# Dilated attention with a head's two segments on separate halves of the partitions

## The chip, the cores and the metric

The kernel runs on one core of one Trainium2 chip. The metric is the device time of one execution in microseconds; the median of several executions is compared. The time before is 3458.81 us, the median of 3 runs (3457.89 to 3460.41).

## What is computed

Sixteen images of 128 channels and 28 x 28 pixels (784 tokens) go through a small hybrid network: two convolution blocks, a softmax attention, a routed block with GELU experts, a dilated attention, and a routed block with SiLU experts. The change is in the dilated attention and in the stage that prepares its operands. For each of 16 heads of 8 channels it computes three things on the tokens, in their order after a permutation:

```python
# tokens 0..255, dilation 1: softmax(q k^T / sqrt(8)) v over 256 tokens
# tokens 256..767, dilation 2: head h takes the 256 tokens of parity h % 2; the others give 0
# tokens 768..783 (all that is left of the third segment), dilation 4:
#                              head h takes the tokens of kind h % 4 (4 of 16)
o = out.transpose(0, 2, 1, 3).reshape(B, S, E)
return o @ w_out + b_out
```

So a head has two "segments" of 256 tokens with 256 x 256 scores each, and a rest of 16 tokens that is computed with a mask.

## The kernel before, in words

**Stage by stage.** `program` runs the stages one after the other on the residual `R`, which stays in SBUF. `dilated_inputs` (L1637) gathers the GELU experts' rows into `R`, normalizes, and multiplies by the q, k and v weights. `dilated_attention` (L1937) then runs the attention, with the routing of the following block woven into the same loop.

**Operands in pieces.** q and k are fp32 values written as three bf16 pieces each. One image's piece is 528 wide (`OWN = 2 * SEG + 16`): segment 0, segment 1 (a head's own parity), and the 16 tokens left. In `dilated_inputs`, TensorE writes the product into the PSUM tile `pqk` (`product`, L1782: two matmuls of 256 columns for parities, one for segment 0, one of 16 columns at L1786), ScalarE makes the first piece (L1849), VectorE the rest (L1907), ScalarE the second piece (L1852), GpSimd the third (L1751), and SyncE stores them to HBM (L1716). Between these, GpSimd gathers expert rows (L1739) and VectorE weighs them (L1866).

**Loads.** The attention works per image on tiles `q[side][g]` and `k_[side][g]`, where g is a group of 8 heads and the side alternates with the image. A tile has 99 partitions: six slots of 8 rows (products of pieces: hi x hi, hi x lo and so on, `Q_SLOTS` and `K_SLOTS`) are rows 0 to 47, rows 48 to 95 are zeros, and rows 96 to 98 hold three pieces of minus the row maximum in q, and ones in k. `load` (L2078) issues 12 DMAs on SyncE's queue for one (image, g), each 8 partitions x 8 heads x 528 elements (L2083). GpSimd zeroes k (L2131), VectorE zeroes q (L2341), ScalarE sets k's rows of ones (L2330).

**Units of one turn.** `steps` (L1953) writes out the order of the work of a turn by hand, for every engine alike; a turn has a step h for each head:

```python
for h in range(D_HEADS):
    score(2 * h)                 # also "weigh" and "take" of a group of 8 scores
    if maxima: out.append(("max", h))
    score(2 * h + 1)
    if maxima and h == 9: out.append(("turn", 0))
    if exps and h == 2:   out.append(("turn", 1))
```

- `score` k (L2191): the transposed scores of one (head, segment), two matmuls of 99 rows and 256 columns into one of three banks `sbank` (L2202), then the exponential on ScalarE (L2304). A bank comes free when its exponential is done. Before the change, unit k is head `4 * (k // 8) + k % 4`, segment `k // 4 % 2`.
- `max` h (L2205): the scores of the next image's head h, both segments, four matmuls of 96 rows (L2212) into one of two double banks `rot`, then a maximum along the rows on VectorE (L2360). Many other small steps share the two `rot` in turn: `turn`, `compact` (L2248), `den` (L2254), `add` (L2286), `rows` (L845, L846), `ranks` (L1008 on), `gate` (L1073), `score16` (L2260), `max16` (L2218), `weigh16` (L2270). TensorE waits for VectorE to free a `rot` before it fills it again (L2190).
- `turn` g (L2221): the maxima's pieces, made by GpSimd (L2146 to L2152), are transposed on TensorE (L2229, L2230), copied to `mt` by VectorE (L2366, L2367), and moved by three DMAs on SyncE into rows 96 to 98 of q (L2116).
- `weigh` gr (L2231): the context of four heads, 16 matmuls in fp32 with 32 output partitions each (L2241), copied by ScalarE (L2320).

A turn computes the scores of image t, the maxima of image t+1, and on SyncE the loads of image t+2: `load 0` at h = 8 and `load 1` at h = 15 (L2117), both behind waits for exponentials. Turn -1 has maxima alone. Score 0 of a turn waits for the max rows of group 0, score 16 and `score16` (at h = 5) for those of group 1. At the start SyncE issues the loads of two images, 48 DMAs, before anything else of its queue (L2090 to L2094).

## Time and profile before

| what | before |
|---|---|
| median of 3 runs | 3458.81 us |
| span of the profiled execution | 3455.1 us |
| what lies around the span, against the median | 3.7 us |
| dilated_inputs, from its first product to its last | 1995 to 2229 us |
| dilated_attention, first instruction to last exponential | 2240.4 to 3013 us |
| one image in the middle of it | 47.78 us |
| busy in such an image: TensorE, VectorE, ScalarE, GpSimd | 39.1, 36.3, 22.9, 28.4 us |

The span runs from the first to the last instruction of the profiled execution, and the sums of this document are made against it. Busy time of TensorE contains modelled pipeline ends, so it is more than what the array needs. Rows of the timeline name the engine (PE = TensorE matmul, PEld = its weight load, DVE = VectorE, ACT = ScalarE, POOL = GpSimd, SPq = SyncE's DMA queue), the line of the kernel, and in brackets how long the engine sat idle before and what released it ("issue": nothing that the profile shows).

### The profile page before, as it was taken

The numbers are of one execution on the slowest core, as the hardware profiler recorded it, in microseconds if no ns is written. First come the engines' busy times: TensorE is split into PE (matmuls) and PEld (weight loads), VectorE is DVE, ScalarE is ACT, GpSimd is POOL, SyncE is SP. The second block draws the span as 40 slices with busy tenths as digits, with TensorE's granted clock in tenths as the row PEclk, the third lists the DMA queues.
The fourth block names the chain that finished last, engine by engine and source line by source line (L and its number), as shares of the span: only waits on it lengthen the run. The fifth ranks groups of instructions, "written<-read, shape, count | busy, mean of one in ns | idle before, by whom it ended". The sixth has DMA issues, their size and how long they took to land. (4 is left out here: it accounts for less than half of the span.)

```text
span 3455.1 us, 64405 instructions
## 1 busy us (share of the span) xinstructions
PE 2842.9 (82%) x20886; PEld 1557.4 (45%) x20887; DVE 2208.0 (64%) x4232; ACT 1550.2 (45%) x3274; POOL 1023.2 (30%) x1344
## 2 busy tenths in 40 slices
PE   6777869999999999999499766578888888739998
PEld 3334523343333433333189655445555555423336
DVE  6774567778777787776222245477777777647662
ACT  1112526566666666666255422254444445414440
POOL 0001311122222222222333346425556565630000
PEclk9998969999999999999799889878898889859995
DMA  2002462223222232230222223332333233031123
GB/s 79 0 0 75 184 130 41 37 41 56 40 52 49 41 52 44 41 59 9 77 62 62 65 77 106 104 77 52 61 60 65 57 66 60 27 108 52 51 59 121
DMA packets 208898, 215.73 MB, mean 62 GB/s; under 512 B 33104, under 2 KB 184848, under 8 KB 208656
## 3 DMA queue, kind: packets, MB, share of 16 engines
q1 hardware_dynamic: 183024, 176.63, 22.3%
q0 software_dynamic: 14336, 25.72, 2.8%
q10 hardware_dynamic: 11312, 10.35, 1.0%
q8 instruction: 144, 2.36, 0.3%
q14 instruction: 82, 0.67, 0.1%
HBM read 129.26 MB, written 81.90 MB: 61 GB/s over the span
## 5 line engine op out<-in xcount | busy, mean ns | idle before, releaser
L1557 ACT ACTIVATE attn_exps<-attn_sbank 128x392 f32<-128x392 f32 x1600 | 705.0, 503 | 468.1 <-PE attn_sbank L1474 463.4
L1602 DVE TENSOR_REDUCE attn_mx<-attn_rot 128x1 f32<-128x784 f32 x768 | 722.4, 967 | 189.7 <-PE attn_rot L1487 186.7
L1487 PE MATMUL attn_rot<-attn_k,attn_q 96*128 96x392 bf16 x1536 | 402.7, 345 | 69.6 <-DVE attn_mx L1602 39.2
L1474 PE MATMUL attn_sbank<-attn_q,attn_k 99*128 99x392 bf16 x1536 | 451.2, 334 | 10.6 <-ACT attn_exps L1557 9.4
L2304 ACT ACTIVATE dil_exps<-dil_sbank 128x512 f32<-128x512 f32 x512 | 289.5, 598 | 365.0 <-PE dil_sbank L2202 361.6
L2360 DVE TENSOR_REDUCE dil_mx<-dil_rot 128x4 f32<-128x1024 f32 x256 | 307.4, 1218 | 74.0 <-PE dil_rot L2212 71.9
L1514 PE MATMUL attn_acc<-attn_exps,attn_v 128*32 128x392 f32 x3584 | 351.1, 503 | 0.0
L1474 PEld LDWEIGHTS attn_sbank<-attn_q,attn_k 99*128 99x128 bf16 x1536 | 149.2, 98 | 269.4 <-ACT attn_exps L1557 134.2
L2678 PE MATMUL silu_ph<-silu_route_w,silu_xT 128*128 x424 | 237.8, 645 | 20.4 <-issue 12.5
L1487 PEld LDWEIGHTS attn_rot<-attn_k,attn_q 96*128 96x128 bf16 x1536 | 117.8, 99 | 276.8 <-DVE attn_mx L1602 179.2
L2212 PE MATMUL dil_rot<-dil_k,dil_q 96*128 96x256 bf16 x1024 | 176.3, 302 | 80.2 <-DVE dil_mx L2360 50.4
L1105 POOL DMA_INDIRECT silu_rows<-silu_route_xt,silu_route_posi x224 | 213.0, 951 | 56.3 <-issue 54.0
L2202 PE MATMUL dil_sbank<-dil_q,dil_k 99*128 99x256 bf16 x1024 | 199.7, 300 | 13.6 <-ACT dil_exps L2304 12.1
L2729 DVE TENSOR_TENSOR silu_acc<-silu_h,silu_acc 128x512 f32 x212 | 146.8, 692 | 78.8 <-issue 46.1
L2702 ACT ACTIVATE silu_h<-silu_ph 128x512 f32<-128x512 f32 x212 | 126.6, 597 | 151.0 <-PE silu_ph L2678 151.0
L1429 POOL TENSOR_TENSOR attn_mx<-attn_mx_left,attn_own 128x4 f32<-128x4 f32 x32 | 6.5, 202 | 593.6 <-DVE attn_mx_left L1602 593.6
L2571 ACT ACTIVATE gelu_hT<-gelu_ph,gelu_wb 128x128 f32<-128x128 f32 x424 | 121.1, 368 | 109.3 <-PE gelu_ph L2545 109.3
L2212 PEld LDWEIGHTS dil_rot<-dil_k,dil_q 96*128 96x128 bf16 x1024 | 92.4, 104 | 158.2 <-DVE dil_mx L2360 92.3
L1514 PEld LDWEIGHTS attn_acc<-attn_exps,attn_v 128*32 128x32 f32 x3584 | 90.6, 109 | 150.5 <-issue 97.4
L2241 PE MATMUL dil_acc<-dil_exps,dil_v 128*32 128x256 f32 x2048 | 148.0, 439 | 1.4 <-ACT dil_exps L2304 1.4
L2593 DVE TENSOR_TENSOR gelu_y<-gelu_py,gelu_wb 128x128 f32<-128x128 f32 x106 | 30.9, 292 | 167.9 <-PE gelu_py L2555 167.9
L188 PE MATMUL conv_pb<-conv_z,conv_cw 96*128 96x392 f32 x192 | 89.3, 629 | 44.0 <-ACT conv_z L217 40.3
(367 smaller groups left out, 4789.8 us busy)
## 6 DMA issues: line engine op xcount, KB each, us to landing
attn_q<-q_pieces SPq DMA_DIRECT2D x192, 98.0 KB, 3.7
attn_k<-k_pieces SPq DMA_DIRECT2D x192, 98.0 KB, 5.1
silu_x<-silu_rows SPq DMA_DIRECT2D x212, 64.0 KB, 1.8
dil_q<-dil_q_pieces SPq DMA_DIRECT2D x192, 66.0 KB
dil_k<-dil_k_pieces SPq DMA_DIRECT2D x192, 66.0 KB
q_pieces<-qkv_piece SPq DMA_DIRECT2D x16, 588.0 KB, 3.1
k_pieces<-qkv_piece SPq DMA_DIRECT2D x16, 588.0 KB, 3.2
v_rows<-qkv_v SPq DMA_DIRECT2D x16, 476.0 KB, 3.8
```

The source lines that it names most:

```text
L1105: pool.indirect_dma_start(self.xs, bass.IndirectOffsetOnAxis(ap=self.posi[im.side][:, k, c:c + 1], axis=0), self.xt[im.side][:, c, :], Non ...
L1474: ins = nc.tensor.matmul(into[:, 0:HS], k_[t.side][g][:, j, c * P:(c + 1) * P], q[t.side][g][:, j, cols], start=True, stop=True)
L1487: ins = nc.tensor.matmul(rot[b][:, hf, 0:HS], q[nxt.side][g][0:QROWS, j, c * P:(c + 1) * P], k_[nxt.side][g][0:QROWS, j, cols], start=True ...
L1514: ins = nc.tensor.matmul(acc[32 * j:32 * j + 32, 0:HS], v[im.side][:, c, at:at + 32], e_[:, (u + (j if c < FULL else 0)) % NP, :], start=( ...
L1557: nc.scalar.activation(e_[:, n % NP, :], sbank[(n + t.side) % 3][:, 0:HS], ACT.Exp, scale=A_DIM ** -0.5).then_inc(s_ex, 1)
L1602: nc.vector.tensor_reduce(into, rot[b][:, :, 0:HS], AX.XY, ALU.max).then_inc(s_free, 1)
L2202: ins = nc.tensor.matmul(sbank[k % 3][:, kc * SEG:(kc + 1) * SEG], k_[t.side][h // 8][:, h % 8, at + kc * P:at + (kc + 1) * P], q[t.side][ ...
L2212: ins = nc.tensor.matmul(rot[b][:, seg, qc * SEG:(qc + 1) * SEG], q[nxt.side][h // 8][0:QROWS, h % 8, at + qc * P:at + (qc + 1) * P], k_[n ...
L2241: ins = nc.tensor.matmul(acc[32 * j:32 * j + 32, seg * SEG:(seg + 1) * SEG], v[im.side][:, 2 * seg + kc, at:at + 32], e_[:, (8 * gr + 4 * ...
L2304: nc.scalar.activation(e_[:, k % NP, :], sbank[k % 3][:], ACT.Exp, scale=D_DIM ** -0.5).then_inc(s_ex, 1)
L2360: nc.vector.tensor_reduce(mx[:, x[1], :], rot[b][:, :, :].rearrange("k s (q n) -> k (s q) n", n=SEG), AX.X, ALU.max).then_inc(s_free, 1)
L2678: nc.tensor.matmul(ph[n][:, :], xT[n][:], w1[:, bass.ds(e, 1), :].rearrange("p o f -> p (o f)"), start=True, stop=True).then_inc(s_ph, 1)
```

## The change

A head's segment 0 goes to partitions 0 to 63 and its segment 1 to partitions 64 to 127 of the q and k tiles. Each half has 48 rows of pieces and 3 rows for maxima or ones; the zero rows are gone. The 16 tokens left are stored behind both segments. Scores use 51 rows and maxima 48 rows of one half, so that each matmul starts at partition 0 or 64. Unit k is now head k // 2, segment k % 2. The loads become 24 DMAs per (image, g) of half the size, and the max rows 6 DMAs in place of 3. GpSimd sets the ones (and the rows that the loads then overwrite) with eight memsets; VectorE's four memsets and ScalarE's four instructions go. In `dilated_inputs` the two segments lie in two PSUM banks, and the product has one more matmul of 16 columns.

```diff
-OWN = 2 * SEG + 16
+HALF = SEG + 16
+OWN = 2 * HALF
...
-        rest = [[m.sb(f"rest{j}{t}", [P, OWN]) for t in two] for j in two]
-        piece = [[m.sb(f"piece{j}{t}", [P, PIECES, OWN], bf16) for t in two] for j in two]
+        rest = [[m.sb(f"rest{j}{t}", [P, 2, HALF]) for t in two] for j in two]
+        piece = [[m.sb(f"piece{j}{t}", [P, PIECES, 2, HALF], bf16) for t in two] for j in two]
...
                 def product(lhs, src, dst):
...
-                    return nc.tensor.matmul(dst[:, 2 * SEG:OWN], lhs[:, 0, :], src[:, 3 * SEG:S], start=True, stop=True)
+                    for seg in two:
+                        ins = nc.tensor.matmul(dst[:, BANK * seg + SEG:BANK * seg + HALF], lhs[:, 0, :], src[:, 3 * SEG:S], start=True, stop=True)
+                    return ins
...
-D_KR = QROWS + MROWS
+D_ROWS = 48
+D_KR = D_ROWS + MROWS
...
-        q = [[m.sb(f"q{s}{g}", [D_KR, 8, OWN], bf16) for g in two] for s in two]
+        q = [[m.sb(f"q{s}{g}", [P, 8, HALF], bf16) for g in two] for s in two]
...
-        LOADS = 16 * 2 * len(Q_SLOTS)
+        LOADS = 16 * 4 * len(Q_SLOTS)
...
                         for r, p in enumerate(slots):
-                            s = src[p, 64 * g:64 * g + 64, bass.ds(img.e, 1), :].rearrange("(h d) b s -> d h (b s)", d=D_DIM)
-                            sp.dma_start(dst[img.side][g][r * D_DIM:(r + 1) * D_DIM, :, :], s).then_inc(s_ld[img.side][g], 16)
+                            for seg in two:
+                                s = src[p, 64 * g:64 * g + 64, bass.ds(img.e, 1), HALF * seg:HALF * (seg + 1)].rearrange("(h d) b s -> d h (b s)", d=D_DIM)
+                                at = 64 * seg + r * D_DIM
+                                sp.dma_start(dst[img.side][g][at:at + D_DIM, :, :], s).then_inc(s_ld[img.side][g], 16)
...
                 for s in two:
                     for g in two:
-                        sp.wait_ge(s_qz, 2 * s + g + 1)
-                        sp.wait_ge(s_kz, 2 * s + g + 1)
+                        sp.wait_ge(s_ones, 2 * s + g + 1)
                         load(Turn(s), g)
...
-                            for r in range(MROWS):
-                                sp.dma_start(q[img.side][g][QROWS + r:QROWS + r + 1, :, :], mt[g][8 * r:8 * r + 8, :]).then_inc(s_mr[g], 16)
+                            for seg in two:
+                                for r in range(MROWS):
+                                    at = 64 * seg + D_ROWS + r
+                                    sp.dma_start(q[img.side][g][at:at + 1, :, :], mt[g][8 * r:8 * r + 8, seg, :]).then_inc(s_mr[g], 16)
...
-                        nc.gpsimd.memset(k_[s][g][0:QROWS, :, :].bitcast(fp32), 0.0).then_inc(s_kz, 1)
+                        for seg in two:
+                            ins = nc.gpsimd.memset(k_[s][g][64 * seg + 32:64 * seg + 64, :, :], 1.0)
+                        ins.then_inc(s_ones, 1)
...
-                            gr, seg, j = k // 8, k // 4 % 2, k % 4
-                            h = 4 * gr + j
...
+                            h, seg = divmod(k, 2)
...
+                            row = slice(64 * seg, 64 * seg + D_KR)
                             for kc in two:
-                                ins = nc.tensor.matmul(sbank[k % 3][:, kc * SEG:(kc + 1) * SEG], k_[t.side][h // 8][:, h % 8, at + kc * P:at + (kc + 1) * P],
-                                                       q[t.side][h // 8][:, h % 8, at:at + SEG], start=True, stop=True)
+                                ins = nc.tensor.matmul(sbank[k % 3][:, kc * SEG:(kc + 1) * SEG], k_[t.side][h // 8][row, h % 8, kc * P:(kc + 1) * P],
+                                                       q[t.side][h // 8][row, h % 8, 0:SEG], start=True, stop=True)
...
-                            for seg in two:
-                                at = SEG * seg
-                                for qc in two:
-                                    ins = nc.tensor.matmul(rot[b][:, seg, qc * SEG:(qc + 1) * SEG], q[nxt.side][h // 8][0:QROWS, h % 8, at + qc * P:at + (qc + 1) * P],
-                                                           k_[nxt.side][h // 8][0:QROWS, h % 8, at:at + SEG], start=True, stop=True)
+                            for qc in two:
+                                for seg in two:
+                                    row = slice(64 * seg, 64 * seg + D_ROWS)
+                                    ins = nc.tensor.matmul(rot[b][:, seg, qc * SEG:(qc + 1) * SEG], q[nxt.side][h // 8][row, h % 8, qc * P:(qc + 1) * P],
+                                                           k_[nxt.side][h // 8][row, h % 8, 0:SEG], start=True, stop=True)
...
-                                ins = nc.tensor.matmul(rot[b][0:16, 0, 16 * h:16 * h + 16], q[nxt.side][h // 8][0:QROWS, h % 8, 2 * SEG:OWN],
+                                ins = nc.tensor.matmul(rot[b][0:16, 0, 16 * h:16 * h + 16], q[nxt.side][h // 8][0:D_ROWS, h % 8, SEG:HALF],
...
-                                                               e_[:, (8 * gr + 4 * seg + j) % NP, kc * SEG:(kc + 1) * SEG], start=(kc == 0), stop=(kc == 1))
+                                                               e_[:, (8 * gr + 2 * j + seg) % NP, kc * SEG:(kc + 1) * SEG], start=(kc == 0), stop=(kc == 1))
...
-                        ins = nc.scalar.activation(k_[s][g][QROWS:D_KR, :, :], zeros[QROWS:D_KR, 0:1].rearrange("p (h s) -> p h s", h=1).broadcast_to([MROWS, 8, OWN]),
-                                                   ACT.Identity, bias=one[QROWS:D_KR, :])
...
-                        nc.vector.memset(q[s][g][0:QROWS, :, :].bitcast(fp32), 0.0).then_inc(s_qz, 1)
...
-                            nc.vector.tensor_copy(mt[x[1]][:, 2 * SEG:OWN], rot[b][0:MROWS * 8, 1, 0:8].bitcast(bf16)).then_inc(s_free, 1)
+                            left = rot[b][0:MROWS * 8, 1, 0:8].bitcast(bf16).rearrange("r (o n) -> r o n", o=1).broadcast_to([MROWS * 8, 2, 16])
+                            nc.vector.tensor_copy(mt[x[1]][:, :, SEG:HALF], left).then_inc(s_free, 1)
```

## Rows read from the trace of the kernel before

**Rows 1.** By stretch: length, then PE, PEld, DVE, ACT, POOL busy, clock, DMA share, GB/s.

```profile
2482.82:2530.61 47.79, 39.14 (x469) 25.19 (x459) 36.31 (x70) 22.92 (x41) 28.39 (x40) 0.89 0.33 61
2530.61:2578.39 47.78, 39.15 (x468) 25.17 (x460) 36.30 (x70) 22.92 (x41) 28.39 (x40) 0.89 0.32 61
...
2541.80:2548.50 6.70, 6.58 (x42) 3.12 (x46) 6.56 (x13) 4.01 (x8) 4.99 (x5) 0.50 0.25 42
2558.90:2562.10 3.20, 3.20 (x43) 1.85 (x47) 1.78 (x3) 0.60 (x1) 1.37 (x2) 0.50 0.38 83
2589.60:2596.30 6.70, 6.57 (x42) 3.11 (x45) 6.56 (x13) 3.98 (x8) 5.01 (x5) 0.50 0.26 54
...
2554.50:2558.00 3.50, 1.48 (x14) 1.08 (x13) 3.36 (x7) 1.57 (x3) 3.05 (x4) 1.00 0.32 55
2586.00:2589.50 3.50, 1.48 (x12) 0.61 (x10) 3.36 (x8) 2.65 (x5) 1.52 (x2) 1.00 0.12 35
```

**Rows 2.** The waits, 2435 to 2913 us: engine, waited for: total us, times, longest.

```profile
PEld dil_rot L2212 <- DVE dil_mx L2360: 59.6, 70, 1.8
DVE dil_mx L2360 <- PE dil_rot L2212: 41.7, 31, 2.4
...
DVE dil_r_xc L864 <- PE dil_rot L846: 17.7, 10, 1.8
```

**Rows 3.** Timeline around a weigh, full clock: start us, us, engine, line, op, idle before.

```profile
2569.51 0.60 PE L2212 MATMUL dil_rot<-dil_k,dil_q 96*128 96x256 bf16 x4
2569.95 0.60 PE L2202 MATMUL dil_sbank<-dil_q,dil_k 99*128 99x256 bf16 x4
2570.48 1.94 PE L2241 MATMUL dil_acc<-dil_exps,dil_v 128*32 128x256 f32 x32
2572.35 0.61 PE L2212 MATMUL dil_rot<-dil_k,dil_q 96*128 96x256 bf16 x4
...
2570.48 1.45 PEld L2241 LDWEIGHTS dil_acc<-dil_exps,dil_v 128*32 128x32 f32 x32 [0.21 <-issue]
2572.34 0.33 PEld L2212 LDWEIGHTS dil_rot<-dil_k,dil_q 96*128 96x128 bf16 x4 [0.41 <-issue]
...
2570.29 1.52 ACT L2304 ACTIVATE dil_exps<-dil_sbank 128x512 f32<-128x512 f32 x3
...
2573.00 1.23 DVE L2360 TENSOR_REDUCE dil_mx<-dil_rot 128x4 f32<-128x1024 f32 x1 [1.37 <-PE dil_rot L2212]
```

**Rows 4.** A weigh at the half clock, the same view.

```profile
2546.17 3.09 PE L2241 MATMUL dil_acc<-dil_exps,dil_v 128*32 128x256 f32 x32
```

**Rows 5.** DMAs of the start and of one load, by window: packets, and q1's packets, MB, share.

```profile
DMA packets 1626, 1.53 MB, mean 128 GB/s; under 512 B 181, under 2 KB 1625, under 8 KB 1625
q1 hardware_dynamic: 1625, 1.53, 56.3%
...
q1 hardware_dynamic: 642, 0.60, 54.7%
```

**Rows 6.** Timeline of SyncE's queue at the start of the stage.

```profile
2242.81 2.08 SPq L2083 DMA_DIRECT2D dil_q<-dil_q_pieces  x6
...
2262.82 3.31 SPq L2083 DMA_DIRECT2D dil_k<-dil_k_pieces  x6
2266.17 0.35 SPq L2086 DMA_DIRECT2D dil_v<-dil_v_rows  x1
2266.57 0.47 SPq L2088 DMA_DIRECT2D dil_v<-dil_v_rows  x1
2269.91 13.99 SPq L2116 DMA_DIRECT2D dil_q<-dil_mt  x6
```

**Rows 7.** Timeline of the start, GpSimd, VectorE and TensorE.

```profile
2240.40 7.25 POOL L2131 MEMSET dil_k<- 96x2112 f32 x4 [10.49 <-POOLq L59]
...
2255.18 1.89 PE L2212 MATMUL dil_rot<-dil_k,dil_q 96*128 96x256 bf16 x8 [26.88 <-DMA dil_k<-dil_k_pieces]
...
2275.97 0.42 PE L2202 MATMUL dil_sbank<-dil_q,dil_k 99*128 99x256 bf16 x1
```

**Rows 8.** SyncE's queue over one image, from its `load 1` on.

```profile
2544.55 2.01 SPq L2083 DMA_DIRECT2D dil_q<-dil_q_pieces  x6
2546.60 2.05 SPq L2083 DMA_DIRECT2D dil_k<-dil_k_pieces  x6
2554.34 2.00 SPq L2116 DMA_DIRECT2D dil_q<-dil_mt  x3
...
2570.46 2.09 SPq L2083 DMA_DIRECT2D dil_q<-dil_q_pieces  x6
2572.59 2.06 SPq L2083 DMA_DIRECT2D dil_k<-dil_k_pieces  x6
2574.69 2.01 SPq L2116 DMA_DIRECT2D dil_q<-dil_mt  x3
```

**Rows 9.** The matmuls that wait for the max rows, timeline of TensorE.

```profile
2564.32 0.56 PE L2260 MATMUL dil_rot<-dil_q,dil_k 99*16 99x16 bf16 x16
```

**Rows 10.** dilated_inputs: the 16-column matmuls and the gather wait, timeline of one image.

```profile
2141.86 0.41 PEld L1786 LDWEIGHTS qkv_d_qk<-qkv_d_xn,qkv_d_w 128*128 128x128 f32 x2
...
2142.70 1.41 PEld L1800 LDWEIGHTS qkv_d_rstd_rows<-qkv_d_rin,qkv_d_spread 128*128 128x128 f32 x10 [0.43 <-DVE qkv_d_rin L1888]
...
2146.51 1.09 DVE L1866 TENSOR_TENSOR qkv_d_yw<-qkv_d_yg,gelu_route_gates 112x896 f32<-112x896 f32 x1 [3.86 <-DMA qkv_d_yg<-gelu_out_rows,gelu_route_positions]
...
2149.04 1.19 POOL L1751 TENSOR_TENSOR qkv_d_piece<-qkv_d_rest,qkv_d_piece 128x528 bf16<-128x528 f32 x1 [4.77 <-ACT qkv_d_piece L1852]
```

51 lines of the change are left out of this document (19 added, 32 removed).

## The prediction

> **What bounds the kernel now.** I read first the busy time by stretch. Two images in the middle of the dilated attention take 47.78 and 47.79 us, with TensorE busy 39.1, VectorE 36.3, ScalarE 22.9 [rows 1]. No engine is full, so the period is a chain that changes hands between TensorE and VectorE through the two `rot` buffers. The waits say in which direction: over ten images TensorE's weight loads for maxima wait 59.6 us for VectorE, and VectorE's reductions wait 41.7 us for TensorE [rows 2]. The first is TensorE being early, and a faster TensorE only lengthens it. The second, 4.2 us an image, and a wait of 1.8 us for the router's matmuls (L864) are where a faster TensorE can help. The timeline shows what the 4.2 us are: three or so gaps an image, each behind a weigh. TensorE runs max 0.60, two scores 0.60, weigh 1.94, then the next max 0.61, and VectorE stands 1.37 us until that max is there [rows 3].
>
> The clock stretches come with every image: 6.7 us and 3.2 us at 0.50, which is the 1.2 GHz level [rows 1]. A weigh there takes 3.09 us in place of 1.94 [rows 3, 4]. In the long one VectorE is busy 6.56 of 6.70 us, so it isn't TensorE that binds there, slow clock or not.
>
> **The change in the steady images.** An image has 32 scores of two matmuls and 16 maxima of four, 128 matmuls of 256 columns. Four of them start within 0.44 us (2569.51 to 2569.95) [rows 3], 0.11 us each. On separate halves a max's four could run as two pairs: 0.22 us saved per max. Of two neighbouring scores the last matmul of one half and the first of the other could run together: 0.11 us. That is at most 16 x 0.33 = 5.3 us of TensorE an image, but only what stands on the chain counts. Behind each of three exposed weighs the max comes 0.22 us earlier. Before the weigh more could be saved, 0.33 to 0.55 us, but there ScalarE does three exponentials back to back in 1.52 us [rows 3], and a score needs the bank of the third score before it: the work before a weigh is paced by ScalarE at 0.51 us a score, and of the saving I count 0.05. Sum: 3 x 0.27 = 0.8 us; the router's block gets its `rot` no earlier, 0.
>
> Against it stands a switch. Going from scores to the weigh, which uses another shape of the array, the weight loads stand 0.21 us with no releaser, and 0.41 us on the way back, where the same loads between scores and maxima run without a gap [rows 3]. With 51- and 48-row scores, the blocks that use all rows (`den`, `add`, `rows`, `ranks`) get such switches too, eight an image. In matmul starts a switch is worth about 0.1 us (the weigh starts 0.53 us after four matmuls that need 0.43). Half of them fall where TensorE waits for VectorE anyway: -0.4 us. Net I take 0.4 us an image. Bounds: -0.4 (switches alone, nothing overlaps) and +2.1 (all of 4 x (0.22 + 0.11 + 0.22), no pacing by ScalarE). Fifteen turns have both scores and maxima: -6 us, between +6 and -31. I take the value near the lower end because the rows that I can follow have VectorE or ScalarE full.
>
> The Trainium skill, "TensorEngine Tiling (Array Packing)", Key Properties, says that tiles can load and multiply in parallel, and that changing the tiling mode drains the engine; Theoretical Speedup gives up to 2x at 64 rows or fewer. By the first half alone TensorE's 128 matmuls would take half their time; the gaps around the weigh agree with the second half. No row here shows two row halves at once.
>
> **The start of the stage.** Here the cost sits. Before, SyncE issues 48 load DMAs from 2242.81 to 2266.13, 0.49 us each, two DMAs for v, and then the group-0 max rows at 2269.91 [rows 6]; the first score follows at 2275.97 [rows 7], right behind the last maxima of turn -1, so these rows had some 2 us of slack. In the middle of this TensorE first waits until 2255.18 for the loads of image 0 [rows 7]. After, SyncE issues 96 DMAs before the same max rows. Each has as many descriptors as before (8 partitions x 8 heads), only shorter, and six are issued in 2.0 to 2.1 us where nothing is queued [rows 8]: 0.345 us each, so 96 take at least 33.1 us. From 2254 to 2266 the transfers run at 56.3% of 16 engines, that is nine of them, 1625 packets in 12 us: 16 x 12 x 0.563 / 1625 = 67 ns a packet of 1056 bytes [rows 5]. A half packet costs between 34 ns (by bytes, then issue binds) and 67 ns (by number). With 768 packets on each of eight engines the second is 51 us. I take 0.40 us per DMA, 38.4 us in all, nearer to the issue bound since 0.345 is what the queue itself shows.
>
> GpSimd's four memsets take 1.85 us each [rows 7]; the first load waits for two new ones (2176 elements wide instead of 2112, on a quarter of the partitions). Between one memset's and two memsets' old time that is 0 to 2 us later: +1.0. VectorE's and ScalarE's setup instructions lay beside this and are worth 0. So the loads are issued by 2243.8 + 38.4 = 2282.2, v's two by 2283.1, and the six max-row DMAs, at 0.67 us each (three in 2.01) [rows 8], by 2287.1; for the landing I put 1 us, an estimate that no row settles. The first score starts at 2288 instead of 2276. **+12 us**, from +6 (issue-bound, quick memsets) to +25 (by number of packets). TensorE executes in order and nothing of turn 0 is in front of score 0, so nothing covers it.
>
> The Trainium skill, "DMA: Bandwidth & Descriptors", Rules for kernel authors, says of two transfers to disjoint partition halves: don't bother, they serialize, use one of 128 partitions. By that rule the halves would gain nothing and the issue time would be paid twice, which is the direction that the sum above has. The issue rows agree; whether half packets are slower per byte no row shows.
>
> **Loads and max rows in the steady images.** `load 1` starts at 2544.55 and is issued in 4.1 us; with 24 DMAs it is 8.3 us, to 2552.9, and the max rows behind it are ready at 2554.34, so they are not held up in the queue [rows 8]. They take 4.0 us instead of 2.0 and reach q around 2560; `score16` needs them at 2564.32 [rows 9]. The transfers are the other bound: 54.7% of 16 engines over 8 us for 642 packets is 109 ns each [rows 5], so 768 packets on eight engines take 10.5 us, and 1536 by number 20.9, until 2566.3: 2 us late. By bytes they end as before. `load 0` at 2570.46 is followed at once by max rows (2574.69); they would go out at 2578.8 and land by 2585, or 2592 by number, and the next image's score 0 comes at 2592.3. I take 0 between 0 and 2 us an image. The cover is a margin of 4 us at `score16`; if the period shrank, it would shrink too.
>
> **dilated_inputs.** One more 16-column matmul in fp32 per product: two weight loads, 0.41 us, twice an image. Behind the k product the next user of TensorE waits 0.43 us anyway, and VectorE then waits 3.86 us for the gather [rows 10]. Four operations are 3% wider (544 for 528); GpSimd's two (1.19 us each) lie in the gather's chain: 0.1 us an image, 1.5 us in all, from 0 to 8 (all of the matmuls exposed in half the images).
>
> **Sum** against the profiled span: 3455.1 + 12 + 1.5 - 6 = 3462.6, and with the 3.7 us around it 3466.3. The median of before stands at 3458.8, so this is +0.2%, at the edge of what a measurement of this kernel can tell from no change (0.2%, 7 us).
>
> **Rivals.**
> - **A. TensorE is the bound after all (faster).** The pairs overlap, the weighs start earlier, and each exposed wait shrinks as in the upper bound: 3455.1 + 12 + 1.5 - 31 + 3.7 = 3441. For it: TensorE has the highest busy time, and 41.7 us of waits for it. Against: ScalarE's row of three exponentials. It decides above 0.9 us an image, where the start is paid back. Chance 0.22.
> - **B. The clock falls more often.** In the stretches before both falls TensorE was busy 1.48 of 3.5 us [rows 1]. A TensorE with less to do has more such stretches. A weigh in one costs 1.15 us more [rows 3, 4]; one more weigh per image at 1.2 GHz gives 3466 + 17 = 3483. For it: the two images have equal periods to 0.01 us, with the falls at the same places, so the period and the clock hold each other. Chance 0.17.
> - **C. Packets cost by number.** +25 at the start, and 0.7 us a turn at `score16`: 3455.1 + 25 + 1.5 - 6 + 10 + 3.7 = 3489. For it: packets in a load take 109 ns in one place and 67 in another, so it is not bytes alone. Against: issue is then no longer the limit. Chance 0.13.
> - **D. The change doesn't do what it says:** the halves don't run together, or what they gain is swallowed by VectorE. Steady images cost 0 to 0.4 us more: 3455.1 + 12 + 1.5 + 3 + 3.7 = 3475. Chance 0.13.
>
> **Chances.** My forecast of 3466 holds 0.35, and its own range, 3455 to 3474, lies across the 0.2% line. Faster by over 0.2%: A and a little of the forecast, 0.25. Within 0.2%: 0.25. Slower: 0.50. The range of 8 in 10 reaches from most of A to most of C: 3438 to 3490.
>
> **What would show it.** In the profile after: the first score (L2202's successor) near 2288 us with SyncE's loads before it as the wait; starts of a max's matmuls in pairs; the wait of `dil_mx` for `dil_rot` falling from 4.2 to about 3.5 us an image, while TensorE's wait for `dil_mx` grows; gaps of 0.2 us around `den`, `add`, `rows`, `ranks`; a period of 47.4. A period under 46.9 makes the forecast wrong on A's side; a first score before 2280 makes the start's term wrong; more than 10 us an image at 0.50 is B; TensorE standing before `score16` for a DMA is C; starts 0.11 us apart in all maxima are D.

## The result, and the profile after

The changed kernel takes 3469.8 us (median of 20 executions) against 3459.9 of the kernel before beside it: ratio 1.0044, interval 1.0024 to 1.0064. It is slower, by 0.44% in this ratio, which goes with the means (it leaves out the slowest execution), and by 0.29% in the medians. The spread says more than the median: the kernel before stays between 3450 and 3468, the changed one runs from 3459 to 3512. Thirteen of its executions have a mean granted clock of 0.887 to 0.891 and a median of 3468.8; seven have 0.869 to 0.882 and a median of 3502. The kernel before has 0.904 to 0.911 in the executions beside the experiments, 69 of them, of which two disturbed ones (4478 and 7202 us) are left out.

The profiled execution after took 3468.8 us, span 3465.8, clock 0.889; before 3455.1 and 0.909. Its 10.7 us more, by place:

| place | before | after | difference |
|---|---|---|---|
| last centring matmul of `dilated_inputs` | 2213.6 | 2215.7 | +2.1 |
| GpSimd's first memset of the stage | 2240.40 | 2243.08 | +2.7 in all |
| first score | 2275.97 | 2287.38 | +11.4 in all |
| start of the last score | 3011.5 | 3027.1 | +15.6 in all |
| end of the span | 3455.1 | 3465.8 | +10.7 |

Of the 2.7 us, 1.1 is there at the first centring matmul (1978.4 and 1979.5), so 1.6 belongs to `dilated_inputs`. One pair of profiles can't tell so little: from the first to the last centring matmul that stage takes between 234.9 and 238.5 us in the six profiles with its code unchanged. The stretch behind the last score is the same code in both kernels; it took 443.6 and 438.7 us here. That -4.9 is not plain scatter. The kernel before and its five variants have 442.9 to 447.1 us there (mean 444.1), the changed kernel and its seven variants 437.6 to 443.4 (mean 440.3). Why, no run here tells.

**The start.** SyncE's queue and TensorE in the changed kernel, the same columns as [rows 6, 7]:

```profile
2246.95 4.16 SPq L2087 DMA_DIRECT2D dil_q<-dil_q_pieces  x12
...
2277.01 4.14 SPq L2087 DMA_DIRECT2D dil_k<-dil_k_pieces  x12
2281.20 0.36 SPq L2090 DMA_DIRECT2D dil_v<-dil_v_rows  x1
2281.60 0.43 SPq L2092 DMA_DIRECT2D dil_v<-dil_v_rows  x1
2282.07 4.12 SPq L2121 DMA_DIRECT2D dil_q<-dil_mt  x6
```

```profile
2257.26 1.04 PE L2217 MATMUL dil_rot<-dil_k,dil_q 48*128 48x256 bf16 x8 [26.55 <-DMA dil_k<-dil_k_pieces]
...
2277.06 0.60 PE L2217 MATMUL dil_rot<-dil_k,dil_q 48*128 48x256 bf16 x4 [0.52 <-DVE dil_mx L2353]
2287.38 0.39 PE L2207 MATMUL dil_sbank<-dil_q,dil_k 51*128 51x256 bf16 x1 [9.72 <-DMA dil_q<-dil_mt]
```

96 loads take 34.2 us to issue, 4.14 us for most groups of twelve, and the max rows wait behind them in the queue: TensorE is done with its maxima and then stands 9.72 us for their DMA.

**The middle images.** By stretch, two images of the changed kernel and then its low-clock stretches and the one ahead of a fall, the columns of [rows 1]:

```profile
2493.99:2541.78 47.79, 36.71 (x460) 21.20 (x459) 36.59 (x69) 22.57 (x41) 28.31 (x40) 0.82 0.25 62
2541.78:2589.57 47.79, 36.74 (x460) 21.20 (x460) 36.59 (x69) 22.57 (x41) 28.34 (x40) 0.82 0.24 62
...
2567.60:2577.80 10.20, 7.15 (x71) 4.06 (x75) 7.82 (x14) 2.52 (x5) 6.18 (x7) 0.50 0.23 68
2557.30:2564.10 6.80, 6.21 (x52) 2.39 (x49) 6.66 (x13) 3.05 (x6) 5.79 (x8) 0.50 0.31 72
2554.00:2557.30 3.30, 1.48 (x13) 0.62 (x14) 3.16 (x8) 3.29 (x6) 0.62 (x1) 1.00 0.10 29
```

The period is that of before to 0.01 us, TensorE is 2.4 us less busy, and the clock is 0.82 where it was 0.89: an image has 17.0 us at 1.2 GHz (10.2 and 6.8) where it had 9.9 (6.7 and 3.2).

**The pairs.** Timeline of TensorE in the changed kernel, at full clock and then at half clock, to set beside [rows 3, 4]:

```profile
2587.18 0.39 PE L2217 MATMUL dil_rot<-dil_k,dil_q 48*128 48x256 bf16 x4
2587.41 0.38 PE L2207 MATMUL dil_sbank<-dil_q,dil_k 51*128 51x256 bf16 x2
...
2590.51 0.28 PE L2207 MATMUL dil_sbank<-dil_q,dil_k 51*128 51x256 bf16 x1
2590.52 0.28 PE L2217 MATMUL dil_rot<-dil_k,dil_q 48*128 48x256 bf16 x1
...
2558.92 0.61 PE L2217 MATMUL dil_rot<-dil_k,dil_q 48*128 48x256 bf16 x4
2559.32 0.63 PE L2207 MATMUL dil_sbank<-dil_q,dil_k 51*128 51x256 bf16 x4
2559.88 3.64 PE L2246 MATMUL dil_acc<-dil_exps,dil_v 128*32 128x256 f32 x32
```

The halves run together: a max takes 0.39 us instead of 0.60, and a score and a max on different halves start 0.01 us apart. The Trainium skill, "TensorEngine Tiling (Array Packing)", Key Properties, says that different tiles can load and multiply in parallel; these rows agree. A weigh that lies at half clock from end to end takes 3.64 us; the 3.09 of [rows 4] began at 2546.17, and the stretch at half clock ended at 2548.5, inside it.

**Where the gain of an image went.** Groups of VectorE's instructions over ten images. The kernel before, 2470.71 to 2948.45 us (behind the bar: busy us, mean ns, then idle before it and its releaser):

```profile
L2360 DVE TENSOR_REDUCE dil_mx<-dil_rot 128x4 f32<-128x1024 f32 x161 | 193.6, 1218 | 43.1 <-PE dil_rot L2212 41.7
L1080 DVE COPY dil_r_gates_t<-dil_rot 16x448 f32<-16x448 f32 (+1 forms) x20 | 10.2, 544 | 0.0
L2369 DVE RECIPROCAL dil_rec<-dil_rot 128x128 f32<-128x128 f32 x10 | 9.6, 958 | 11.2 <-PE dil_rot L2248 11.2
L1059 DVE TENSOR_TENSOR dil_r_w<-dil_r_w,dil_r_dfe 112x7 f32<-112x7 f32 x10 | 8.6, 859 | 0.3
L1053 DVE TENSOR_SCALAR dil_r_den<-dil_r_dfe 112x7 f32<-112x7 f32 x10 | 2.6, 260 | 0.0
```

The changed kernel, 2485.49 to 2963.40 us:

```profile
L2353 DVE TENSOR_REDUCE dil_mx<-dil_rot 128x4 f32<-128x1024 f32 x161 | 193.6, 1218 | 38.8 <-PE dil_rot L2217 37.4
L1053 DVE TENSOR_SCALAR dil_r_den<-dil_r_dfe 112x7 f32<-112x7 f32 x10 | 11.2, 1118 | 0.0
L1080 DVE COPY dil_r_gates_t<-dil_rot 16x448 f32<-16x448 f32 (+1 forms) x20 | 10.3, 548 | 4.4 <-PE dil_rot L1073 4.4
L2363 DVE RECIPROCAL dil_rec<-dil_rot 128x128 f32<-128x128 f32 x10 | 9.6, 958 | 8.7 <-PE dil_rot L2253 8.7
L1059 DVE TENSOR_TENSOR dil_r_w<-dil_r_w,dil_r_dfe 112x7 f32<-112x7 f32 x10 | 2.1, 206 | 0.3
```

The gain is there, and it is given back within the image. Over ten images VectorE waits 4.3 us less for the maxima and 2.5 less for `compact`. It waits 4.4 us more for the router's gate transposes (L1073), which lie at half clock now: the seven of an image take 1.48 us where they took 0.85. And the small operations `dil_r_den` and `dil_r_w` (13.3 us together for 11.2 before) take 2.1 more: `dil_r_den`, 112 x 7 elements, takes 1.12 us for 0.26, `dil_r_w` 0.21 for 0.86. Sum: -6.8 and +6.5 us, over ten images.

Why these two operations change is in the timeline. The first two lines are of the kernel before, the last two of the changed one, each time `dil_r_den` and GpSimd's addition beside it:

```profile
2554.24 0.15 DVE L1053 TENSOR_SCALAR dil_r_den<-dil_r_dfe 112x7 f32<-112x7 f32 x1
2554.31 1.27 POOL L2178 TENSOR_TENSOR dil_o_sum<-dil_o_sum,dil_o_part 128x512 f32<-128x512 f32 x1
...
2568.82 1.12 DVE L1053 TENSOR_SCALAR dil_r_den<-dil_r_dfe 112x7 f32<-112x7 f32 x1
2568.66 1.26 POOL L2186 TENSOR_TENSOR dil_o_sum<-dil_o_sum,dil_o_part 128x512 f32<-128x512 f32 x1
```

Where GpSimd's addition starts 0.06 us behind `dil_r_den`, it takes 0.15 us; where it starts 0.17 us ahead of it, `dil_r_den` lasts until 0.02 us behind the addition's end. So it is in all sixteen images of both traces: `dil_r_den` or `dil_r_w` is long only when such an addition is already running, and then ends 0.02 us behind it.

The copy behind the router's matmuls (L864 behind L846), which the experiments come back to, waits 18.0 us over these ten images in both kernels.

### The profile page after: what moved, and what is told of

It reads as the page before. It is cut to its first block and busy times, and to the rows that moved or that the text cites. A ratio compares the mean times of both kernels' runs of the same rounds, so it can differ in the third digit from the quotient of the medians.

```text
span 3465.8 us, 65002 instructions
## 1 busy us (share of the span) xinstructions
PE 2815.1 (81%) x20950; PEld 1504.6 (43%) x20951; DVE 2206.4 (64%) x4226; ACT 1530.7 (44%) x3270; POOL 1034.2 (30%) x1348
## 5 line engine op out<-in xcount | busy, mean ns | idle before, releaser
L2207 PE MATMUL dil_sbank<-dil_q,dil_k 51*128 51x256 bf16 x1024 | 189.5, 312 | 36.5 <-ACT dil_exps L2309 22.3
L2217 PE MATMUL dil_rot<-dil_k,dil_q 48*128 48x256 bf16 x1024 | 128.7, 316 | 94.6 <-DVE dil_mx L2353 66.4
L2246 PE MATMUL dil_acc<-dil_exps,dil_v 128*32 128x256 f32 x2048 | 167.3, 483 | 1.4 <-ACT dil_exps L2309 1.4
L2501 POOL COPY gelu_wb<-gelu_route_w1b 128x644 f32 x106 | 76.6, 724 | 163.7 <-DVE gelu_y L2587 148.2
```

Source lines behind the costliest of these rows:

```text
L2207: ins = nc.tensor.matmul(sbank[k % 3][:, kc * SEG:(kc + 1) * SEG], k_[t.side][h // 8][row, h % 8, kc * P:(kc + 1) * P], q[t.side][h // 8][ ...
L2246: ins = nc.tensor.matmul(acc[32 * j:32 * j + 32, seg * SEG:(seg + 1) * SEG], v[im.side][:, 2 * seg + kc, at:at + 32], e_[:, (8 * gr + 2 * ...
```

## The experiments

All twelve share the kernel before as reference (medians 3458.0, 3460.8 and 3459.0 in the three sets). A period below is that of an image in the middle of the stage. Because the stage begins at another time in each execution, the first score is counted from the last centring matmul of `dilated_inputs` (L1783): 62.4 us in the kernel before, 71.7 in the changed one.

**1. Half-sized loads alone.** The kernel before, each load cut in two by columns:

```diff
-  sp.dma_start(dst[...][g][r * D_DIM:(r + 1) * D_DIM, :, :], s).then_inc(...)
+  for part in two:
+      cols = slice(OWN // 2 * part, OWN // 2 * (part + 1))
+      s = src[p, 64 * g:64 * g + 64, bass.ds(img.e, 1), cols].rearrange(...)
+      sp.dma_start(dst[...][g][r * D_DIM:(r + 1) * D_DIM, :, cols], s).then_inc(...)
```

> The kernel before with each load DMA cut in two by columns (264 and 264 elements), everything else as before: full-height matmuls, 12 us of nothing else. Theory 1: the first score comes 8 to 12 us later than the 2276.0 us of before and the time is +8 to +12 us (0.25 to 0.35%), so that it stands near the changed kernel; middle images stay at 47.8 us with the 1.2 GHz part at 10.2 us an image. Rival (packets cost by number and delay max rows in each image): middle images get longer than 48.5 us.

Measured: 3465.5, ratio 1.0025 (1.0013 to 1.0036). The first score comes at 72.2 us, +9.8. Timeline of its start, SyncE and then TensorE:

```profile
2248.57 4.17 SPq L2085 DMA_DIRECT2D dil_q<-dil_q_pieces  x12
...
2286.12 2.10 SPq L2118 DMA_DIRECT2D dil_q<-dil_mt  x3
...
2291.50 0.59 PE L2204 MATMUL dil_sbank<-dil_q,dil_k 99*128 99x256 bf16 x2 [4.63 <-DMA dil_q<-dil_mt]
```

From first to last score it takes 736.1 us, against 735.5 before: in the images the doubled loads cost nothing. So the doubled number of loads alone is enough for the start's loss. (The changed kernel's first score lies +9.3 in the same count, with later memsets and six max-row DMAs as well; here those rows took 3.3 us to land, there 1.2, so the parts don't match one by one.)

**2. The order of the first loads.** The changed kernel, with the last of the four first loads (image 1, group 1) issued behind the first max rows:

```diff
-  load(Turn(s), g)
+  if (s, g) != (1, 1):
+      load(Turn(s), g)
   ...
   sp.dma_start(q[img.side][g][at:at + 1, :, :], mt[...]).then_inc(s_mr[g], 16)
+  if t.lo < 0:
+      load(Turn(1), 1)
```

> The changed kernel with the last of the four initial loads (image 1, heads 8 to 15, 24 DMAs) issued behind the first max rows instead of before them. Theory 1 (SyncE's issue of 96 loads holds the first score back): the first score starts about 8 us earlier (24 x 0.347) than the 2287.4 us of the changed kernel, near 2279 to 2280, and the time falls by 6 to 8 us, to about the kernel before. Rival (the loads' transfers, not their issue, or the maxima, hold it): the first score moves by less than 3 us. Middle images stay at 47.8 us by both.

Measured: the first score at 63.1 us, 8.6 earlier, but a median of 3469.7 (1.0042, 1.0012 to 1.0073). Of its twelve executions six have a clock of 0.889 or more and a median of 3456.2; the other six have 0.867 to 0.881 and 3488.6. The start was won, as theory 1 had it, and in the median it was lost to the executions at the lower clock. This pointed away from the queues.

**3. Two queues for the first loads.** The changed kernel, the k half of the first loads on ScalarE's queue:

```diff
-  load(Turn(s), g)                 # SyncE
+  load(Turn(s), g, q)              # SyncE, q alone
+  act.wait_ge(s_ones, 2 * s + g + 1)
+  act.dma_start(k_[s][g][at:at + D_DIM, :, :], src).then_inc(s_ld[s][g], 16)
```

> The changed kernel with the k half of the initial loads issued on ScalarE's queue, where ScalarE only waits for its first score. Theory 1: SyncE is through its 48 loads 16.6 us earlier, and the first score is then held by the chain of maxima instead: it starts near 2275 to 2278, 9 to 12 us earlier than 2287.4; time -8 to -12 us, a little below the kernel before. Rival (the eight DMA engines are the limit): less than 4 us.

Measured: the first score at 64.1 us, 7.6 earlier; 3464.8, ratio 1.0045 (1.0022 to 1.0068). Seven executions at 0.888 or more with a median of 3462.8, five at 0.875 to 0.880 with 3489.9. The same picture. One thing is hidden by the place that I count from: `dilated_inputs` ahead of it, from first to last centring matmul, took 240.3 us in this profile at a clock of 0.85, and 236.2 at 0.88 in the changed kernel. Experiment 12, which has the same edit, shows 240.6. No other profile is over 238.5.

**4. The rows alone.** The kernel before with 48 rows in place of 96 for maxima and 51 in place of 99 for scores, both segments from partition 0 as before, loads whole. The rows left out hold zeros:

```diff
-D_KR = QROWS + MROWS
+D_ROWS = 48
+D_KR = D_ROWS + MROWS
-  matmul(rot[b][...], q[...][0:QROWS, ...], k_[...][0:QROWS, ...])
+  matmul(rot[b][...], q[...][0:D_ROWS, ...], k_[...][0:D_ROWS, ...])
```

> The kernel before with the zero rows dropped: maxima with 48 rows and scores with 51, but both segments on partitions 0 to 63, so no two halves can work at once; loads whole, as before. Theory 2 (the shape alone costs only the switches; what changes the clock is the work done in pairs): four matmuls of a max still start 0.11 us apart, middle images at 47.8 us or up to 0.4 us more, the 1.2 GHz part near 10 us. Rival (matmuls in a 64-row shape keep the clock lower by themselves): the 1.2 GHz part of a middle image rises toward the 17 us of the changed kernel without any overlap. Time: before -2 to +8 us.

Measured: 3554.6, ratio 1.0267 (1.0244 to 1.0291), the largest effect of the study, and not the -2 to +8 us that I had written; the rival on record, that the shape by itself keeps the clock lower, holds. (Its profiled execution, 3563.1, stands 27 us behind already ahead of the stage, which the change does not touch; from first to last score it takes 812.6 us for 735.5.) Two images in the middle, by stretch, and TensorE's timeline in one:

```profile
2514.93:2566.43 51.50, 45.41 (x460) 29.23 (x459) 36.40 (x70) 23.00 (x41) 28.36 (x39) 0.74 0.29 57
2566.43:2620.80 54.37, 49.82 (x461) 31.34 (x460) 37.18 (x70) 23.33 (x41) 28.33 (x39) 0.67 0.23 54
```

```profile
2593.50 1.06 PE L2214 MATMUL dil_rot<-dil_k,dil_q 48*128 48x256 bf16 x4
2594.35 1.06 PE L2204 MATMUL dil_sbank<-dil_q,dil_k 51*128 51x256 bf16 x4
...
2604.88 0.61 PE L2214 MATMUL dil_rot<-dil_k,dil_q 48*128 48x256 bf16 x4 [0.20 <-DVE dil_mx L2356]
```

The matmuls are as many and as long as before at full clock (0.61 for a max), but the clock is 0.67 to 0.74 in these two images, and 0.64 in a later one of 54.76 us, instead of 0.89. TensorE is no less busy, it is busier, because more of its matmuls run at half clock. So in this kernel the number of rows in use goes with the granted clock, and at half clock TensorE's chain (1.06, 1.06, without a gap) is the bound. Whether it is the rows themselves or the smaller tile of the array that the clock goes with, this run doesn't part. The change uses the same numbers of rows, so I take it that it has this loss in it and that the pairs win most of it back (0.82); no run splits the two.

**5. The pairs taken out of a max.** The changed kernel, a max's matmuls segment by segment, not in turn:

```diff
-  for qc in two:
-      for seg in two:
+  for seg in two:
+      for qc in two:
```

> The changed kernel with the maximum's matmuls ordered segment by segment (half 0, half 0, half 1, half 1) instead of alternating. Theory (only neighbours of different halves overlap): one of four starts is shared instead of two, a max takes 0.50 us at full clock instead of 0.39. Middle images at 47.8 us all the same.

Measured: 3474.4, a single execution, so without an interval. A max still takes 0.40 to 0.41 us, not the expected 0.50, so the edit doesn't take the overlap away: the second segment's first matmul joins the first segment's last. For the pairs this is inconclusive. But its profile has what the changed kernel's own shows only early in the stage, the lower clock. By stretch, four images in a row:

```profile
2574.63:2622.44 47.81, 36.81 (x460) 21.34 (x459) 36.59 (x70) 22.56 (x41) 28.37 (x39) 0.82 0.23 62
2622.44:2670.23 47.79, 36.80 (x460) 21.39 (x459) 36.58 (x70) 22.56 (x41) 28.37 (x39) 0.82 0.25 62
2670.23:2719.13 48.90, 40.15 (x460) 24.17 (x459) 36.53 (x70) 22.67 (x41) 28.37 (x39) 0.76 0.25 61
2719.13:2770.40 51.27, 42.87 (x460) 25.10 (x459) 36.65 (x70) 22.68 (x41) 28.37 (x39) 0.70 0.23 58
```

The same instructions on the same data go from 47.79 to 51.27 us, with the clock from 0.82 to 0.70. The largest part of what the image pays is for one block. VectorE's groups in an image of 47.86 us and in that of 51.27:

```profile
L864 DVE COPY dil_r_xc<-dil_rot 112x512 f32<-112x512 f32 x1 | 0.7, 693 | 1.8 <-PE dil_rot L846 1.8
...
L864 DVE COPY dil_r_xc<-dil_rot 112x512 f32<-112x512 f32 x1 | 0.7, 692 | 3.9 <-PE dil_rot L846 3.9
```

The matmuls that it waits for, in the same two images:

```profile
2494.37 0.45 PE L845 MATMUL dil_rot<-dil_r_center,main_resid 128*112 128x128 f32 x2
...
2738.61 0.75 PE L845 MATMUL dil_rot<-dil_r_center,main_resid 128*112 128x128 f32 x2
```

In the pattern that gives 47.79 the router's fp32 matmuls (L845, L846) run at full clock. When they lie at half clock, VectorE waits 2.1 us more for them; 1.3 us more of waits for the maxima make up the rest of the 3.4. In the changed kernel's own long image, 2387.09 to 2437.56, this wait is 4.2 us for 1.8, nearly all that it has over the next image (50.47 for 47.93).

**6. A busier TensorE.** The changed kernel, each max's four matmuls issued twice, 64 matmuls an image of work for nothing:

```diff
-  for qc in two:
+  for qc in (0, 1, 0, 1):
```

> The changed kernel with each maximum's four matmuls issued twice (the same result twice), so that they take as long as before the change. Theory 2: TensorE's time here is not what binds, and more work keeps the clock up: the 1.2 GHz part of a middle image falls from 17.1 toward the 10.2 us of before, and the time changes by less than 7 us either way. Rival (overlap of the halves does pay, and its loss shows): middle images get longer by 0.5 us or more, +8 us or more.

Measured: 3466.4, ratio 1.0017 (1.0005 to 1.0029), and all twelve executions at a clock of 0.895 to 0.900, 3459.7 to 3475.1. By stretch, an image early in the stage and one of the middle:

```profile
2384.96:2432.88 47.92, 38.80 (x525) 24.18 (x524) 36.43 (x70) 22.59 (x41) 28.37 (x39) 0.86 0.24 62
...
2576.34:2624.13 47.79, 38.87 (x524) 24.29 (x523) 36.41 (x70) 22.67 (x41) 28.36 (x39) 0.86 0.23 63
```

In the changed kernel the corresponding image still takes 50.47 us at 0.73:

```profile
2387.09:2437.56 50.47, 41.66 (x460) 24.44 (x459) 36.60 (x70) 22.56 (x41) 28.39 (x39) 0.73 0.22 59
```

More work makes the kernel no slower, takes the executions over 3476 away, and brings the stretch from first to last score back to 735.5 us (739.7 in the changed kernel, 735.5 before). The period stays at 47.79, though TensorE is 2.1 us busier. This is the run that tells rival B from D: swallowed gains alone would have left the executions as they were.

**7. Dummy work in one place.** The changed kernel, 16 matmuls into `acc` ahead of `gate`, behind a wait for the last `take`:

```diff
+  if x[0] == "gate" and t.lo < B:
+      pe.wait_ge(s_o, 4 * t.e)
+      for _ in range(16):
+          nc.tensor.matmul(acc[:, 0:SEG], k_[t.side][0][0:D_KR, 0, 0:P], q[t.side][0][0:D_KR, 0, 0:SEG], ...)
```

> The changed kernel with 16 more matmuls (51 rows, 256 columns, result never read) on TensorE ahead of the gate's wait for VectorE, where it stands idle 2.1 us in each image. Theory 2 (the gain was lost to the clock: TensorE that has less to do is given 1.2 GHz for 17.1 us of each image instead of 10.2): the 1.2 GHz stretch around gate, compact and the first weigh shrinks or goes, the weigh behind it takes 1.94 us instead of 2.63, and a middle image gets shorter than 47.79 by 0.5 to 3.4 us (time -7 to -50 us). Rival (the clock doesn't matter, VectorE binds): the clock rises but the period stays at 47.8. Second rival (dummies only delay): period longer by up to 1.7 us.

Measured: 3491.1, ratio 1.0083 (1.0066 to 1.0100), all six executions at 0.879 to 0.881. The images take either 48.2 or 50.9 us with the clock at 0.82 and 0.73, longer than even the second rival had it. So work as such doesn't hold the clock. Here it stands in a block, in front of a step that others wait for, and its own wait may have moved TensorE's order too. I can't part these two, and the run shows only that the place matters.

**8. More for VectorE.** The kernel before, one more reduction of 512 elements an image (0.68 us), in front of that of head 14:

```diff
+  if x[0] == "max" and x[1] == 14 and t.lo >= 0:
+      nc.vector.tensor_reduce(spare[...], rot[b][:, 0, 0:512]..., AX.X, ALU.max)
```

> The kernel before with one more reduction of 512 elements on VectorE in each image, at the last maxima, where VectorE is busy without a gap: about 0.6 us of work. Theory 3 (the image's period and the clock hold each other, small changes are swallowed): the period stays at 47.78 us and the time within 3 us of before. Rival (VectorE's work adds up plainly): period 48.4 us, time +9 us.

Measured: 3469.5, ratio 1.0022 (1.0009 to 1.0034). The period leaves 47.78: 48.05, 48.11, 50.07 and 48.32 follow each other, 48.6 in the mean, +0.85 for +0.68 of work; the clock goes down to 0.83 in the long ones. Theory 3 missed and the rival came close: work added at this place is not swallowed, it shows in full.

**9 and 10. Less for VectorE.** Two of sixteen reductions an image over half of the keys, in the changed kernel (9) and in the kernel before (10). This part of the maxima is left out. Each such reduction takes 0.68 us instead of 1.22.

```diff
+  n = SEG // 2 if x[1] in (6, 14) else SEG
-  tensor_reduce(mx[:, x[1], :], rot[b]...rearrange("k s (q n) -> k (s q) n", n=SEG), ...)
+  tensor_reduce(mx[:, x[1], :], rot[b]...rearrange("k s (q n) -> k (s q) n", n=SEG)[:, :, 0:n], ...)
```

> The changed kernel with two of sixteen reductions of the maxima an image (heads 6 and 14) over half of the keys; this part of the maxima is left out. It takes some 1.1 us of VectorE's work from each image. Theory VectorE paces the image (as an added reduction of 0.6 us gave 0.9 us more a period): period 46.7 to 47.2, total 9 to 16 us less, 3454 to 3460. Rival, the period is held by the place of the clock's falls, whatever TensorE and VectorE do within a microsecond: 47.79 again with 17.1 us at 0.50, and no more than 2 us less in all.

> The same two halved reductions in the kernel before, the same part left out. Theory VectorE paces: period 46.7 to 47.2, 3442 to 3450. Rival, the clock's places hold the period: 47.78 again with 10.2 us at 0.50, 3457. If this one gains and the changed kernel with the same edit gains more, the faster maxima of the row halves count once VectorE has room; if it gains more than the changed kernel, the lower clock eats them.

Measured, in the kernel before: 3449.3, ratio 0.9973 (0.9958 to 0.9989), the clock at 0.902 to 0.908. In the changed kernel: 3483.8, ratio 1.0061 (1.0038 to 1.0084), with all four executions at 0.874 to 0.878. The same 1.1 us less of work make the kernel before 10 us faster and the changed one no faster. Its median is 14 us above the changed kernel's 3469.8, but that was measured in another set, these are four executions, and the intervals of the two ratios overlap (1.0024 to 1.0064 without the edit), so that it is slower isn't shown. By stretch, an image of the kernel before with this edit:

```profile
2511.17:2558.97 47.80, 39.71 (x461) 25.74 (x460) 36.05 (x70) 22.86 (x41) 28.38 (x39) 0.86 0.34 61
```

and four in a row of the changed kernel with it:

```profile
2486.34:2535.80 49.46, 41.23 (x460) 25.50 (x459) 36.18 (x70) 22.67 (x41) 28.34 (x39) 0.72 0.24 61
2535.80:2585.73 49.93, 41.56 (x460) 24.74 (x459) 36.16 (x70) 22.49 (x41) 28.38 (x39) 0.73 0.26 60
2585.73:2633.27 47.54, 39.02 (x460) 22.23 (x459) 36.11 (x70) 22.60 (x41) 28.36 (x39) 0.75 0.23 63
2633.27:2680.94 47.67, 37.96 (x461) 21.93 (x460) 36.12 (x70) 22.60 (x41) 28.37 (x39) 0.79 0.26 63
```

Neither theory on record holds as it stood. The kernel before keeps 47.79 in its middle images, as the rival had it (it gains in the first three, 117.6 us from first score to first score for 124.6), but at a clock of 0.86, not 0.89. Over ten of its middle images the reductions take 10.2 us less, and as in the changed kernel that is given back: 5.4 us by a small operation beside GpSimd that got longer (L938), 3.9 us by waits for the gate transposes, 2.1 us by waits for the maxima, against 3.6 us less of waits for `compact` and `den`. The changed one doesn't keep the period: it finds no pattern that repeats from image to image, only one over four, 48.65 us in the mean, and the copy behind L846 waits 32.1 us over ten images instead of 18.0.

**11. TensorE's work in the kernel before.** Each max's matmuls issued twice there, 0.43 us more a max:

```diff
-  for seg in two:
+  for seg in (0, 1, 0, 1):
```

> The kernel before with the eight... four matmuls of every max issued twice, 64 more matmuls an image, 0.43 us more per max at full clock, 7 us more of TensorE an image. If TensorE were what the period waits for (41.7 us of VectorE's waits over ten images), a good part of it shows: 3 to 7 us an image, 45 to 100 us in all. If VectorE is the pace and a busier TensorE only holds its clock, less than 10.2 us an image at 0.50, period 47.8 to 48.5, and 3458 to 3468. I expect something between: a max now takes 1.03 us at full clock where VectorE's reduction is of the same size, so maxima in a row would be paced by TensorE: period 49 to 50, 3480 to 3495.

Measured: 3504.8, ratio 1.0125 (1.0105 to 1.0146), clock 0.922 to 0.930. The images take 49.33 to 50.97 us, the clock in them is 0.93 to 1.00. That is a little more than expected. By the count of matmuls 7 us more of TensorE cost some 3 us an image; the rest goes into its waits and into the higher clock. So TensorE has some room before the change, though not 7 us of it; this is the case against rival A from the other side.

**12. Both remedies together.** The changed kernel with experiments 3 and 6 in one.

> The changed kernel with two edits together: the k half of the first loads goes out on ScalarE's queue, and the four matmuls of every max are issued twice. So far the first alone moved the first score 7.6 us closer to the end of the stage before (64.1 us behind its last centre matmul, against 71.7) and left executions at a granted clock of 0.875 to 0.880 with times up to 3492; the second alone kept all twelve executions at 0.895 to 0.900, and none over 3475. If the two losses of the change are the start and the executions in which the clock falls more, they add up: first score 64 us behind the last centre matmul, every execution at 0.895 or above, period 47.79, a median of 3466.4 less 8, 3458, so equal to the kernel before within 0.1%. Rival, the start is paid back elsewhere (as in the run with only the order of the loads changed, whose median didn't move): a median near 3466.

Measured: 3460.7, ratio 1.0006 (0.9995 to 1.0017), eleven executions at 0.897 to 0.902, 3454.7 to 3466.2. The first score comes 65.1 us behind the last centring matmul. By the medians the two losses of the change add up and are both undone, as expected. What is left is no gain: the version that is free of both stands level with the kernel before. No version with the row halves beat it. The profile doesn't close this account by place: in its execution (3464.5, above the median) first to last score take 740.8 us, not the 735.5 of experiment 6, nearly all of it in the first three images, so a part of the earlier start went there.

## Why the prediction was right or wrong

The forecast of 3466.3 is 3.5 us under the median of 3469.8, and slower by over 0.2% had the largest chance, 0.50. The start holds in its mechanism, `dilated_inputs` is too small to be told; the third term was wrong, and so was the reason behind it. That the sum came out close is luck.

**The start (+12 us).** Right in its mechanism, and a third too large. From the stage's first memset the first score took 44.3 us for 35.6, +8.7. The issue was 0.356 us a DMA, not 0.40: nothing of it is bound by the packets, so the issue bound was the value to take. The memsets gave +1.5 for the +1.0, the max rows 4.1 us and their landing 1.2, as written. Experiment 1 shows the term by itself (+9.8). That the kernel before had some 2 us of slack there was right: its group-0 max rows were all issued by 2272.00, and with a landing of 1.2 us they were there 2.8 us before the first score. So was that nothing of turn 0 covers the start. (Two small slips changed nothing: the four old memsets are 1.81 us each by [rows 7], not 1.85, and the upper bound of an image adds up to 2.2, not 2.1.)

The Trainium skill, "DMA: Bandwidth & Descriptors", Rules for kernel authors, says of two transfers to disjoint partition halves not to bother. At the start the trace agrees with the advice, though what it shows as the cost is the issue of twice the DMAs, where the page's reason is that both halves share the same engines; in the images they cost nothing (experiment 1).

**`dilated_inputs` (+1.5).** +1.6 in this pair of profiles, inside what the stage varies by itself, so the term is neither shown nor refuted. GpSimd's two operations are 1.22 us for 1.19, 1 us over sixteen images.

**The loads in the images (0).** Right: rival C is out. `score16` waited for a DMA once, 1.2 us in all sixteen images, and experiment 1 has no loss there.

**The steady images (-6 us).** This is the step that failed: "Net I take 0.4 us an image". The parts of it were there. The maxima are 0.21 us shorter, for 0.22; VectorE waits 4.3 us less over ten images for them, and 2.5 less for `compact`; and TensorE's weight loads for maxima wait 77.2 us for VectorE where they waited 59.6. The switches that I priced at 0.4 us an image hardly show: weight loads that stand with no releaser do so for 61.3 us over ten images, for 58.9, and none of them before `den`, `add`, `rows` or `ranks`. What was missing is that the period didn't follow: 47.79 before and after, and 47.79 again with 64 matmuls more (experiment 6), or with 1.1 us less of VectorE in the kernel before (10). I had written "the period and the clock hold each other" as a reason for rival B and not drawn the conclusion for my own term. In the middle of the stage both savings of about a microsecond or less that I tried (the change itself and experiment 10) showed as more time at half clock and not as a shorter image, while added work did lengthen it (experiment 8). I summed savings along the chain at a fixed clock; the clock was not fixed.

**Rival B, the clock.** Its mechanism came true, its price not. More than 10 us an image at 0.50 was the sign for B, and there are 17. But the added half clock falls where TensorE waits anyway: only the gate transposes and the weigh pay (0.6 and 0.8 us an image of TensorE), and the image is no longer. What costs is something that I hadn't seen: the pattern is easily left. Two executions of five (18 of the 44 of the changed kernel and of experiments 2 and 3) have a lower clock and up to 50 us more. None of these 18 was the profiled one. That in them images take 50 to 51 us for a while, because the router's fp32 matmuls fall at half clock, is read from experiment 5's profile (clock 0.882 in all) and from experiments 7 and 9, and not shown for them. Experiments 4, 6 and 12 show the link with the clock from both sides. Why one execution leaves the pattern and the next doesn't, no run here tells.

**Rival D** was wrong in its first half (the halves do run together) and right in its second for the executions that keep the pattern: the gain is swallowed, although not by VectorE's reductions but by the transposes at half clock and the small operations that wait for GpSimd's additions to end. **Rival A** is out: 41.7 us of waits for TensorE's maxima looked like room for 2.1 us an image, of which 0.4 was won for the maxima and kept for none of the image.

**The net.** +8.7 and +1.6 and +4.2 from first to last score (of which 2.8 is the image that took 50.47) against -4.9 behind the last score gives the profile's 10.7 with the 1.1 ahead of it. The forecast came out close because its errors lay on both sides. From first to last score it was 10.2 us too low (-6 for +4.2); against that stood a start 3.3 us too large and the -4.9 behind the stage, for which it had no term. The median owes little to the executions at the lower clock (the thirteen others alone have 3468.8); the ratio of 1.0044 does. The range of 3438 to 3490 holds the median, but not the four slowest executions (3502 to 3512).

## What to carry to other kernels

Where images repeat with the falls of TensorE's clock at the same places, don't add up savings on TensorE at a fixed clock: look at the granted clock by image, and ask which step moves into the half clock when TensorE has less to do, or fewer rows in use. Judge such a kernel by the spread of its executions beside their clock, not by one profile; the profile of the changed kernel here belongs to the better part of them. Count DMAs on the queue ahead of the first transfer that someone waits for, at what one issue takes, before splitting a load; moving half of them to another queue gave 7.6 of the 9.3 us back at that place, though the stage ahead was 4 us longer in both profiles with that edit.

## What the runs showed of the hardware that was not expected

- Fewer rows, lower clock: with 96 and 99 rows the middle images had a granted clock of 0.89, with 48 and 51 rows, the same number of matmuls and the same length at full clock 0.64 to 0.74, and TensorE's busy time went up from 39.1 to between 45.4 and 50.9 us an image.
- The same period in nine kernels (the one of experiment 5 before it leaves it): 47.78 to 47.80 us with TensorE busy 36.7, 38.9, 39.1 and 39.7 us and VectorE 36.05 to 36.6, at a clock of 0.82 to 0.89. Out of the pattern most images take 48 to 51.4 us, and 51.5 to 54.8 with the rows of experiment 4.
- Work that does nothing can steady a kernel: with the doubled maxima none of 23 executions (experiments 6 and 12) was over 3476 us, where 18 of 44 without them had the lower clock and up to 3512 us.
- Row halves need no alternation to overlap: segment by segment a max takes 0.40 us, in turn 0.39.
- A VectorE operation on 112 x 7 elements takes 0.15 to 1.26 us, by its place beside GpSimd's work: when an addition of GpSimd (1.0 to 1.3 us) is already running, it ends 0.02 us behind that addition. The Trainium skill, "SBUF — State Buffer", section SBUF: two separate sides, says that the port pair shared by the two engines is an exclusive lock for a whole instruction, taken by whichever starts first. The ends in the trace agree with that; no run here moved GpSimd's work to test it.
